# Last stage of a graph kernel: GpSimd turns the sums around, ScalarE works in place

## The chip, the cores and the metric

The kernel runs on one core of a Trainium2 chip. The metric is device time in microseconds (us) of one execution. Five engines are spoken of: TensorE (PE, with its weight loads PEld), VectorE (DVE), ScalarE (ACT), GpSimd (POOL), and SyncE (SP), which here only issues DMAs.

## The reference

For 16 batches b, 1024 nodes u and v and 256 features, the reference computes a gate for every pair of nodes and batch, and sums messages with it:

```
pre_u = einsum('bud,dk->buk', h, W1[:d]);  pre_v = einsum('bvd,dk->bvk', h, W1[d:])
hidden = relu(pre_u[:, :, None, :] + pre_v[:, None, :, :] + b1)
S   = sigmoid(einsum('buvk,ko->buvo', hidden, W2)[..., 0] + b2[0])
a_t = einsum('buv,bud->bvd', S * A, h)
m_t = einsum('uv,bud->bvd', A, h) * h
z_t = beta1 * h + beta2 * (a_t @ Wa + ba) + beta3 * (m_t @ Wm + bm)
```

The adjacency A is sparse (about one pair in sixteen is an edge), so the sum over k is only computed for edges.

## The kernel before

Four stages run one after the other, with barriers between them. A node stage computes per-node rows, the products h·Wa (`hWa_dram`), the terms beta1·h + m_t·Wm + biases (`base_dram`) and, per node and batch, a part u and a part v of the gate's argument (`linear_dram`). A small stage then makes lists of indices. The edge loop (256 blocks) computes for each edge and batch a sum of absolute values and scatters it into `sum_dram`, whose layout is [u, v, b] with the 16 batches innermost. A branch for adjacency matrices with crowded blocks follows, which is skipped with these inputs. The last stage turns the sums into gates and multiplies.

The last stage has 64 steps k: 8 column tiles vt of 128 nodes v, and in each 8 row tiles t of 128 nodes u. A step handles one block of 128 x 128 pairs and all 16 batches:

- SP loads the sums of the block into `raw` (1 MB, [u, v, b]), and a block of adj into `adj_b`. At t = 0 it loads `of_v` first, the part v of the tile, broadcast to all partitions (1 MB). In the first column tile it also loads `hWa_all` (2 MB a step), which then stays. At t = 4 it loads `z` from `base_dram` (2 MB), once the store of the `z` of the column tile before has landed (`z_stored`). SP is one queue in the order of the program: a wait in it holds all loads behind.
- GpSimd adds `of_v` to `raw` in place (L1453), one contiguous instruction over 2048 numbers a partition.
- ScalarE applies the sigmoid with 16 instructions (L1510), one a batch. Each reads `raw[:, :, b]`, 128 numbers that lie 16 numbers (64 bytes) apart, with the scale `half_sign` and the bias `of_u[:, t, b]` from SBUF, and writes `masked[:, b, :]`, 128 numbers in a row.
- VectorE multiplies `masked` by `adj_b` in place (L1471), 2048 numbers a partition.
- TensorE multiplies with 16 matmuls in float32 (L1489; each shows as two MATMUL records), and sums over t in all 8 banks of PSUM (`z_psum`).

After the mask of step t = 1, VectorE adds the eight banks of the column tile before to `z` (L1462, `finish`), and only after that may TensorE begin t = 0 of the new tile in each bank. ScalarE's queue issues the store of `z` after the instructions of t = 3 (`store`, L1501).

The buffers: RAW = 3 `raw` buffers, each free for the next load when ScalarE has read it (`gate_made`); GM = 3 `masked` buffers, each free when TensorE has read it (`step_done`, waited for by ScalarE); ADJ = 5 `adj_b` buffers. `of_u` and `of_v` belong to the last stage, and `of_u` is prepared by one VectorE instruction (L1465) before ScalarE may begin. Between the edge loop and the branch stands `finish_step`: a barrier, 29 semaphores cleared one by one on SP, and a second barrier.

Of the kernel before, what the change touches and what calls it, by code (L numbers as in the profile page):

```python
# [5 lines left out]
def gnn_edges_kernel(nc, x, adj, W1, b1, W2, b2, Wa, ba, Wm, bm, beta1, beta2, beta3, out):  # L6
# [15 lines left out]
    ALU = mybir.AluOpType  # L22
# [4 lines left out]
    P = 128  # L27
# [38 lines left out]
    with ctx:  # L66
# [22 lines left out]
        betas = sb("betas", [P, 4])  # L89
        half_sign = sb("half_sign", [P, 1])  # L90
        work = ctx.enter_context(ExitStack())
        ident = sb("ident", [P, P], scope=work)
# [38 lines left out]
        with ExitStack() as phase:  # L131
# [734 lines left out]
            with ExitStack() as part:  # L866
                at_u = sb("at_u", [P, NBLK], scope=part)
                at_v = sb("at_v", [P, NBLK], scope=part)
                empty = sb("empty", [P, TILES, P], scope=part)
                found = sb("found", [P, TILES, P], scope=part)  # L870
                levels = over_scan[0:1, 0:PASSES]
                most = sb("most", [1, NT + 2], scope=part)
                with nc.Block() as block:
                    @block.gpsimd
                    def _(pool):
                        nc.gpsimd.iota(at_u[:], pattern=[[P, NT], [0, NJ], [UB, 2]], base=-1, channel_multiplier=0,
                                       allow_small_or_imprecise_dtypes=True).then_inc(at_made, 1)
                        nc.gpsimd.iota(at_v[:], pattern=[[0, NT], [VB, NJ], [0, 2]], base=0, channel_multiplier=0,
                                       allow_small_or_imprecise_dtypes=True).then_inc(at_made, 1)
                        nc.gpsimd.iota(levels, pattern=[[SLOTS, PASSES]], base=0, channel_multiplier=0,  # L880
                                       allow_small_or_imprecise_dtypes=True).then_inc(at_made, 1)
# [11 lines left out]
                    def _(dve):  # L893
# [17 lines left out]
                        dve.wait_ge(at_made, 3)  # L911
                        link_idx(STT(out=at_u[:], in0=at_u[:], scalar=float(N), in1=at_v[:], op0=ALU.mult, op1=ALU.add))
                        dve.wait_ge(flipped, 1)
                        for k in range(2):
                            turned_ = wide[:, k * SLOTS:(k + 1) * SLOTS].rearrange("p (t n) -> p t n", t=TILES)
                            base_ = at_u[:, k * P:(k + 1) * P].rearrange("p (a n) -> p a n", a=1).broadcast_to([P, TILES, P])
                            link_idx(TS(empty[:], turned_, 0.0, FAR, ALU.is_equal, ALU.mult))
                            link_idx(TT(found[:], turned_, base_, ALU.add))
                            link_idx(TT(found[:], found[:], empty[:], ALU.add))
                            link_idx(nc.vector.tensor_copy(idx_all[:, :, k * P:(k + 1) * P], found[:]))  # L920
                        left_indices(dve, link_idx, left_found, left_u[:], left_v[:], left_at[:], left_base[:], LEFT)
# [7 lines left out]
                    def _(sp):  # L929
# [26 lines left out]
        scattered = [sem(f"scattered{i}") for i in range(RING_S)]  # L956
        edge_sems = [*v_loaded, *u_loaded, *pick_loaded, filled_d, filled_a, drained_d, drained_a, left_set, left_added,
                     left_d, left_a, left_totalled, *first_loaded, signed, totalled, mixed_done]

# [20 lines left out]
        def left_step(n):  # L980

            return n // SPAN - 1, n % SPAN

        with ExitStack() as phase:
# [22 lines left out]
            with nc.Block() as block:  # L1007
                @block.sync
                def _(sp):
# [33 lines left out]
                    for n in range(n_blk):  # L1043
                        waits(sp, filled_d, ND * n)
                        waits(sp, filled_a, NA * n)
                        if n + PKS - 1 < n_blk:
                            load_pick(n + PKS - 1)
                        if n >= VG:
                            k, jj = (n - 1) // VG + 1, (n - 1) % VG
                            if k % ST == TURN * jj and k < ST * NGRP:  # L1050
                                load_v(k, jj)
                        if n % VG == 0 and n // VG + 1 < n_blk // VG:
                            load_u(n // VG + 1)
                    for i in range(RING_S):
                        sp.wait_ge(scattered[i], 16 * TILES * ((n_blk - i + RING_S - 1) // RING_S))
# [122 lines left out]
                def _(pool):  # L1178
# [34 lines left out]
                    for n in range(n_blk):  # L1213
# [31 lines left out]
                        for t in range(TILES):  # L1245
                            col = block_of(*blocks[n])
                            scatter(total[slot][:, t, :], idx_all[:, t, col:col + 1], scattered[slot])
            finish_step(edge_sems)

# [140 lines left out]
        with ExitStack() as phase:  # L1390
            RAW, GM, ADJ = 3, 3, 5
            hWa_all = sb("hWa_all", [P, NT, B, D], scope=phase)
# [3 lines left out]
            z = sb("z", [P, B, D], scope=phase)  # L1396
            of_u = sb("of_u", [P, NT, B], scope=phase)
            of_v = sb("of_v", [P, P, B], scope=phase)
            z_psum = [pb(f"z_psum{i}", [P, BANK], scope=phase) for i in range(B // 2)]
# [3 lines left out]
            u_ready = sem("u_ready")  # L1403
            of_u_loaded = sem("of_u_loaded")
            of_v_loaded = sem("of_v_loaded")
            raw_added = sem("raw_added")
# [18 lines left out]
            with nc.Block() as block:  # L1425
                @block.sync
                def _(sp):
                    sp.dma_start(of_u[:], linear_dram[0, :, :].rearrange("(t p) b -> p t b", p=P)).then_inc(of_u_loaded, 16)  # L1428
                    for vt in range(NT):
                        for t in range(NT):  # L1430
                            k = vt * NT + t
                            if t == 0:
                                waits(sp, raw_added, k)
                                sp.dma_start(of_v[:].rearrange("p v b -> p (v b)"), linear_dram[1, vt * P:(vt + 1) * P, :]  # L1434
                                             .rearrange("(a v) b -> a (v b)", a=1).broadcast_to([P, P * B])).then_inc(of_v_loaded, 16)
                            waits(sp, gate_made, k - RAW + 1)
                            sp.dma_start(raw[k % RAW][:], sum_uv[t * P:(t + 1) * P, vt * P:(vt + 1) * P, :]).then_inc(raw_loaded[k % RAW], 16)
# [9 lines left out]
                def _(pool):  # L1447
                    for vt in range(NT):
                        pool.wait_ge(of_v_loaded, 16 * (vt + 1))
                        for t in range(NT):  # L1450
                            k = vt * NT + t
                            pool.wait_ge(raw_loaded[k % RAW], 16 * (k // RAW + 1))
                            nc.gpsimd.tensor_tensor(raw[k % RAW][:], raw[k % RAW][:], of_v[:], ALU.add).then_inc(raw_added, 1)  # L1453

# [43 lines left out]
                def _(act):  # L1498
# [5 lines left out]
                    for vt in range(NT):  # L1504
                        for t in range(NT):
                            k = vt * NT + t
                            act.wait_ge(raw_added, k + 1)
                            step_done(act, k - GM)
                            for b in range(B):
                                last = nc.scalar.activation(masked[k % GM][:, b, :], raw[k % RAW][:, :, b], ACT.Sigmoid,  # L1510
                                                            bias=of_u[:, t, b:b + 1], scale=half_sign[:, 0:1])
# [32 lines left out]
```

## Time and profile before

| | us |
|---|---|
| median of 3 runs | 4033.04 |
| lowest, highest | 4028.12, 4033.12 |
| profiled execution, its own time | 4027.79 |
| its span | 4026.0 |
| PE busy in it | 3470.5 (86%) |
| DVE busy | 2815.8 (70%) |
| ACT busy | 2435.3 (60%) |
| POOL busy | 1837.0 (46%) |

The busy shares are means over stages with different limits. The last stage is what lies behind the first load at 3362.90 us, so 663 us of the span, and is read by itself below. "Idle before" in a row is the time in which the engine did nothing before the instruction, and the arrow names what ended it.

### The profile page before, as it was taken

The page shows a single profiled execution, that of the slowest core. Times are in us where ns is not written, and L with a number is a line of the kernel's source. Part 1 is how long each engine was busy: PE and PEld are TensorE (multiplying, and loading weights), DVE is VectorE, ACT ScalarE, POOL GpSimd, SP SyncE. Part 2 cuts the span into 40 slices and gives each one's busy share as a digit, 9 for nine tenths or more (in the row PEclk, how much of TensorE's full clock was granted, in tenths as well). Part 3 has the DMA queues.
Part 4 walks back from the last instruction along what each step waited for, and adds up shares of the span by engine and source line. Part 5 has one row for each costly group of instructions (what it writes and reads, how often), then busy time and mean ns, then how long its engine had stood idle before and what let it go on. Part 6 is the DMA issues. An engine that isn't in the chain of part 4 may idle for free. (4 is left out here: it accounts for less than half of the span.)

```text
span 4026.0 us, 56126 instructions
## 1 busy us (share of the span) xinstructions
PE 3470.5 (86%) x14232; PEld 2680.2 (67%) x14232; DVE 2815.8 (70%) x4788; ACT 2435.3 (60%) x14050; POOL 1837.0 (46%) x2338
## 2 busy tenths in 40 slices
PE   4977778887878759999999999999999995687877
PEld 2655555555545548887888888888888884566766
DVE  4455655555554359999999999999999993334333
ACT  0111111111111149998999999999999996788786
POOL 2222212212221126666666666666666654554453
PEclk9988989898989879999999999999999997888988
DMA  4455544555555495666757675666666556654643
GB/s 156 176 185 190 194 167 178 207 186 185 194 187 206 156 220 145 138 150 157 170 143 176 145 177 144 160 159 158 152 147 158 140 113 207 226 183 162 213 177 129
DMA packets 342892, 685.83 MB, mean 170 GB/s; under 512 B 38782, under 2 KB 252648, under 8 KB 319720
## 3 DMA queue, kind: packets, MB, share of 16 engines
q1 hardware_dynamic: 304544, 612.07, 52.5%
q0 software_dynamic: 21504, 53.31, 4.4%
q10 hardware_dynamic: 16512, 16.78, 1.2%
q8 instruction: 116, 1.90, 0.2%
q14 instruction: 216, 1.77, 0.2%
HBM read 444.01 MB, written 256.18 MB: 174 GB/s over the span
## 5 line engine op out<-in xcount | busy, mean ns | idle before, releaser
L1160 ACT ACTIVATE junk<-psum_a 128x128 f32<-128x128 f32 x6144 | 1611.3, 298 | 233.1 <-PE psum_a L1064 149.8
L1160 ACT ACTIVATION_READ_ACCUMULATOR junk<-psum_a 128x1 f32 x6144 | 1385.1, 228 | 0.0
L1105 DVE TENSOR_REDUCE group_sum<-psum_d 128x56 f32<-128x896 f32 x1024 | 1112.6, 1086 | 84.3 <-PE psum_d L1064 41.6
L1063 PE MATMUL psum_d<-u_t,pk 128*128 128x512 f32 x2560 | 1007.3, 393 | 58.9 <-DMA v_t<-rows_dram 33.3
L1064 PE MATMUL psum_d<-v_t,pk 128*128 128x512 f32 x2560 | 1001.2, 391 | 0.0
L1489 PE MATMUL z_psum<-hWa_all,masked 128*128 128x256 f32 x2048 | 486.4, 402 | 183.5 <-DVE masked L1471 128.1
L1209 POOL DMA_INDIRECT sum_dram<-total,idx_all x512 | 506.9, 990 | 228.0 <-POOL total L1220 124.1
L1063 PE MATMUL psum_a<-u_t,pk 128*128 128x512 f32 x1536 | 606.8, 395 | 0.0
L1063 PEld LDWEIGHTS psum_d<-u_t,pk 128*128 128x128 f32 x2560 | 483.0, 189 | 182.2 <-issue 46.2
L1064 PE MATMUL psum_a<-v_t,pk 128*128 128x512 f32 x1536 | 600.0, 391 | 0.0
L1489 PEld LDWEIGHTS z_psum<-hWa_all,masked 128*128 128x128 f32 x2048 | 414.0, 203 | 255.9 <-DVE masked L1471 133.6
L1510 ACT ACTIVATE masked<-raw,of_u,half_sign 128x128 f32<-128x128 f32 x1024 | 510.7, 603 | 116.1 <-POOL raw L1453 78.9
L1064 PEld LDWEIGHTS psum_d<-v_t,pk 128*128 128x128 f32 x2560 | 483.1, 189 | 98.9
L847 POOL TENSOR_TENSOR own<-whole 128x256 f32<-128x256 f32 x128 | 92.6, 724 | 998.2 <-issue 732.2
L601 PE MATMUL wide<-adj_sb,h 128*128 128x512 f32 x1024 | 513.1, 624 | 0.0
L1471 DVE TENSOR_TENSOR masked<-masked,adj_b 128x2048 f32<-128x2048 f32 x64 | 202.5, 3164 | 405.8 <-ACT masked L1510 405.8
L671 ACT COPY hWa<-ring 128x512 f32<-128x512 f32 x64 | 37.5, 587 | 716.1 <-PE ring L623 716.1
L1453 POOL TENSOR_TENSOR raw<-raw,of_v 128x2048 f32<-128x2048 f32 x64 | 303.9, 4764 | 333.4 <-DMA raw<-sum_dram 333.4
L1202 POOL TENSOR_TENSOR fold<-group_sum,group_sign 128x256 f32<-128x256 f32 x256 | 190.2, 743 | 390.9 <-DVE group_sum L1132 387.8
L585 PE MATMUL ring<-W_k,hT 128*128 128x258 f32 x1024 | 276.6, 430 | 104.7 <-ACT whole L664 103.2
L1102 DVE TENSOR_REDUCE late_sum<-psum_d 128x4 f32<-128x512 f32 x512 | 348.0, 680 | 0.8 <-PE psum_d L1064 0.8
L1063 PEld LDWEIGHTS psum_a<-u_t,pk 128*128 128x128 f32 x1536 | 289.4, 188 | 78.9 <-ACT junk L1160 21.4
(207 smaller groups left out, 4049.8 us busy)
## 6 DMA issues: line engine op xcount, KB each, us to landing
u_t<-rows_dram SPq DMA_DIRECT2D x126, 1024.0 KB
rows_dram<-split SPq DMA_DIRECT2D x128, 512.0 KB, 3.3
sum_dram<-zero SPq DMA_DIRECT2D x128, 512.0 KB, 4.9
pk<-pick_dram SPq DMA_DIRECT2D x512, 128.0 KB
raw<-sum_dram SPq DMA_DIRECT2D x64, 1024.0 KB, 6.9
v_t<-rows_dram SPq DMA_DIRECT2D x36, 1024.0 KB
whole_dram<-whole SPq DMA_DIRECT2D x128, 256.0 KB, 3.6
pick_dram<-pick SPq DMA_DIRECT2D x128, 256.0 KB, 2.0
```

Source lines behind the costliest of these rows:

```text
L585: last = nc.tensor.matmul(ring[:, w * BANK:w * BANK + CW], hT[:, c, t * P:(t + 1) * P], W1_k[:, c, w, :], start=(c == 0), stop=(c == DT - 1))
L601: last = nc.tensor.matmul(wide[:, c * N + n * BANK:c * N + (n + 1) * BANK], h[b % 2][:, t, c * P:(c + 1) * P], adj_sb[:, t, n * BANK:(n + ...
L1063: nc.tensor.matmul(dst, pk[n % PKS][:, at:at + P], part(u_t[k % 2][:], b, LB), start=True, stop=False)
L1064: return nc.tensor.matmul(dst, pk[n % PKS][:, SLOTS + at:SLOTS + at + P], part(v_t[n % VG][:], b, LB), start=False, stop=True)
L1102: return nc.vector.tensor_reduce(out_, in_, AX, ALU.add, apply_absolute_value=True)
L1105: nc.vector.tensor_reduce(out_[:, :, 1:EG], in_[:, :, GW:LATE].rearrange("p b (g k) -> p b g k", k=GW), AX, ALU.add, apply_absolute_value= ...
L1160: last = nc.scalar.activation(junk[:, a % RING_A, k * LATE:(k + 1) * LATE], psum_a[a % RING_A][:, k * LATE:(k + 1) * LATE], ACT.Abs, accum ...
L1209: nc.gpsimd.indirect_dma_start(out=sum_dram[:, :], out_offset=bass.IndirectOffsetOnAxis(ap=at, axis=0), in_=sums, in_offset=None, bounds_c ...
L1453: nc.gpsimd.tensor_tensor(raw[k % RAW][:], raw[k % RAW][:], of_v[:], ALU.add).then_inc(raw_added, 1)
L1471: nc.vector.tensor_tensor(masked[k % GM][:], masked[k % GM][:], adj_b[k % ADJ][:].rearrange("p (a v) -> p a v", a=1).broadcast_to([P, B, P ...
L1489: last = nc.tensor.matmul(z_psum[b // 2][:, (b % 2) * D:(b % 2 + 1) * D], masked[k % GM][:, b, :], hWa_all[:, t, b, :], start=(t == 0 and ...
L1510: last = nc.scalar.activation(masked[k % GM][:, b, :], raw[k % RAW][:, :, b], ACT.Sigmoid, bias=of_u[:, t, b:b + 1], scale=half_sign[:, 0:1])
```

## The change

The change has three parts.

1. In the last stage GpSimd reads `raw` and `of_v` in the order [b, v] (128 numbers that lie 64 bytes apart, for each of 16 batches), adds them, and writes `masked[:, b, :]` in runs. ScalarE then works in place on `masked`, in rows. A `raw` buffer is free when GpSimd has read it, and there are 2 of them; of `masked` there are 4, and it is GpSimd, not ScalarE, that waits for TensorE to have read the buffer.
2. `of_u` and `of_v` live from the start of the kernel, and SP loads them in the edge loop, eight blocks before its end. To make room in the stage of indices, four temporary tensors there lie in buffers that exist already (`edge`).
3. After the edge loop there is one barrier in place of barrier, clears and barrier.

```diff
+        of_u = sb("of_u", [P, NT, B])
+        of_v = sb("of_v", [P, P, B])
...
+        def load_of_v(sp, vt):
+            sp.dma_start(of_v[:].rearrange("p v b -> p (v b)"), linear_dram[1, vt * P:(vt + 1) * P, :]
+                         .rearrange("(a v) b -> a (v b)", a=1).broadcast_to([P, P * B])).then_inc(of_v_loaded, 16)
...
+                        if n == n_blk - 2 * VG:
+                            sp.dma_start(of_u[:], linear_dram[0, :, :].rearrange("(t p) b -> p t b", p=P)).then_inc(of_u_loaded, 16)
+                            load_of_v(sp, 0)
...
-            finish_step(edge_sems)
+            nc.all_engine_barrier()
...
-            RAW, GM, ADJ = 3, 3, 5
+            RAW, GM, ADJ = 2, 4, 5
...
-                    sp.dma_start(of_u[:], linear_dram[0, :, :].rearrange("(t p) b -> p t b", p=P)).then_inc(of_u_loaded, 16)
                     for vt in range(NT):
                         for t in range(NT):
                             k = vt * NT + t
-                            if t == 0:
-                                waits(sp, raw_added, k)
-                                sp.dma_start(of_v[:].rearrange("p v b -> p (v b)"), linear_dram[1, vt * P:(vt + 1) * P, :]
-                                             .rearrange("(a v) b -> a (v b)", a=1).broadcast_to([P, P * B])).then_inc(of_v_loaded, 16)
-                            waits(sp, gate_made, k - RAW + 1)
+                            if t == 0 and vt:
+                                sp.wait_ge(raw_added, k)
+                                load_of_v(sp, vt)
+                            waits(sp, raw_added, k - RAW + 1)
                             sp.dma_start(raw[k % RAW][:], sum_uv[t * P:(t + 1) * P, vt * P:(vt + 1) * P, :]).then_inc(raw_loaded[k % RAW], 16)
...
                             pool.wait_ge(raw_loaded[k % RAW], 16 * (k // RAW + 1))
-                            nc.gpsimd.tensor_tensor(raw[k % RAW][:], raw[k % RAW][:], of_v[:], ALU.add).then_inc(raw_added, 1)
+                            step_done(pool, k - GM)
+                            nc.gpsimd.tensor_tensor(masked[k % GM][:], raw[k % RAW][:].rearrange("p v b -> p b v"),
+                                                    of_v[:].rearrange("p v b -> p b v"), ALU.add).then_inc(raw_added, 1)
...
                             act.wait_ge(raw_added, k + 1)
-                            step_done(act, k - GM)
                             for b in range(B):
-                                last = nc.scalar.activation(masked[k % GM][:, b, :], raw[k % RAW][:, :, b], ACT.Sigmoid,
+                                last = nc.scalar.activation(masked[k % GM][:, b, :], masked[k % GM][:, b, :], ACT.Sigmoid,
                                                             bias=of_u[:, t, b:b + 1], scale=half_sign[:, 0:1])
```

How the instructions stand on GpSimd at the start of the last stage (the names of the waits are semaphores: `raw_loaded` is a landed load, `gate_used` a step that TensorE has read). Before:

```order
L1446 UNCONDITIONAL_BRANCH
L1453 TENSOR_TENSOR raw<-raw,of_v 128x2048 [waits raw_loaded0,of_v_loaded]
L1453 TENSOR_TENSOR raw<-raw,of_v 128x2048 [waits raw_loaded1]
L1453 TENSOR_TENSOR raw<-raw,of_v 128x2048 [waits raw_loaded2]
L1453 TENSOR_TENSOR raw<-raw,of_v 128x2048 [waits raw_loaded0]
L1453 TENSOR_TENSOR raw<-raw,of_v 128x2048 [waits raw_loaded1]
```

and now, on GpSimd at the same place:

```order
L1449 UNCONDITIONAL_BRANCH
L1457 TENSOR_TENSOR masked<-raw,of_v 128x2048 [waits raw_loaded0,of_v_loaded]
L1457 TENSOR_TENSOR masked<-raw,of_v 128x2048 [waits raw_loaded1]
L1457 TENSOR_TENSOR masked<-raw,of_v 128x2048 [waits raw_loaded0]
L1457 TENSOR_TENSOR masked<-raw,of_v 128x2048 [waits raw_loaded1]
L1457 TENSOR_TENSOR masked<-raw,of_v 128x2048 [waits gate_used,raw_loaded0]
```

The addition now writes `masked`, uses two `raw` buffers in turn, and from the fifth step on also waits for TensorE.

On SP, where the edge loop ends and the last stage begins (the branch that is skipped left out). Before:

```order
L1019 DMA u_t<-rows_dram 64x4096 x2
L1007 UNCONDITIONAL_BRANCH [waits filled_d,filled_a,scattered0,scattered1,scattered2,scattered3,left_scattered]
L83 ISA [waits barrier_Pool_Activation_PE_DVE_SP_release]
L83 ISA x28
L1426 COMPARE_AND_BRANCH [waits barrier_Pool_Activation_PE_DVE_SP_release]
...
L1428 DMA of_u<-linear_dram 128x8x16
L1434 DMA of_v<-linear_dram 128x2048
L1437 DMA raw<-sum_dram 128x2048
L1439 DMA adj_b<-in_adj_dram 128x128
L1441 DMA hWa_all<-hWa_dram 128x16x256
```

and now, on SP at the same place:

```order
L1025 DMA u_t<-rows_dram 64x4096 x2
L1061 DMA of_u<-linear_dram 128x8x16
L987 DMA of_v<-linear_dram 128x2048
L1013 UNCONDITIONAL_BRANCH [waits filled_d,filled_a,scattered0,scattered1,scattered2,scattered3,left_scattered]
L1431 COMPARE_AND_BRANCH [waits barrier_Pool_Activation_PE_DVE_SP_release]
...
L1440 DMA raw<-sum_dram 128x2048
L1442 DMA adj_b<-in_adj_dram 128x128
L1444 DMA hWa_all<-hWa_dram 128x16x256
```

The two loads have moved ahead of the barrier, and the 29 clears and one barrier are gone.

On SP around t = 4 of a later column tile (z is the load that waits for the store). Before:

```order
L1437 DMA raw<-sum_dram 128x2048 [waits gate_made]
L1439 DMA adj_b<-in_adj_dram 128x128 [waits gate_masked]
L1444 DMA z<-base_dram 128x16x256 [waits z_stored]
L1437 DMA raw<-sum_dram 128x2048 [waits gate_made]
L1439 DMA adj_b<-in_adj_dram 128x128 [waits gate_masked]
```

and now, on SP at the same place:

```order
L1440 DMA raw<-sum_dram 128x2048 [waits raw_added]
L1442 DMA adj_b<-in_adj_dram 128x128 [waits gate_masked]
L1447 DMA z<-base_dram 128x16x256 [waits z_stored]
L1440 DMA raw<-sum_dram 128x2048 [waits raw_added]
L1442 DMA adj_b<-in_adj_dram 128x128 [waits gate_masked]
```

The order of the loads is the same; only the semaphore for which the load of `raw` waits is another.

## Rows read from the trace of the kernel before

**Rows 1.** The page's groups of the last stage: form, count, busy, mean ns, idle before.
```profile
L1489 PE MATMUL z_psum<-hWa_all,masked 128*128 128x256 f32 x2048 | 486.4, 402 | 183.5 <-DVE masked L1471 128.1
L1510 ACT ACTIVATE masked<-raw,of_u,half_sign 128x128 f32<-128x128 f32 x1024 | 510.7, 603 | 116.1 <-POOL raw L1453 78.9
L1471 DVE TENSOR_TENSOR masked<-masked,adj_b 128x2048 f32<-128x2048 f32 x64 | 202.5, 3164 | 405.8 <-ACT masked L1510 405.8
L1453 POOL TENSOR_TENSOR raw<-raw,of_v 128x2048 f32<-128x2048 f32 x64 | 303.9, 4764 | 333.4 <-DMA raw<-sum_dram 333.4
```

**Rows 2.** Timeline of ScalarE's queue: three of the stores. Start, us, instruction.
```profile
3488.51 0.42 ACTq L1501 DMA_DIRECT2D out_dram<-z  x1
...
3959.29 0.38 ACTq L1501 DMA_DIRECT2D out_dram<-z  x1
...
4018.13 0.38 ACTq L1501 DMA_DIRECT2D out_dram<-z  x1
```

**Rows 3.** Busy time in one cycle of eight steps.
```profile
core 0: us, PE busy (x) PEld busy (x) DVE busy (x) ACT busy (x) POOL busy (x), PEclk, DMA share, GB/s
3800.20:3878.80 78.60, 60.44 (x258) 51.52 (x257) 30.56 (x16) 63.80 (x129) 38.28 (x8) 0.89 0.51 181
```

**Rows 4.** Timeline of that cycle, all engines: start, us, instruction, count, idle before.
```profile
3800.19 2.58 ACT L1510 ACTIVATE masked<-raw,of_u,half_sign 128x128 f32<-128x128 f32 x5 [5.31 <-PE z_psum L1489]
3802.30 0.38 ACTq L1501 DMA_DIRECT2D out_dram<-z  x1
...
3809.81 0.37 SPq L1444 DMA_DIRECT2D z<-base_dram  x1
...
3821.10 13.47 POOL L1453 TENSOR_TENSOR raw<-raw,of_v 128x2048 f32<-128x2048 f32 x3 [24.77 <-DMA raw<-sum_dram]
3825.65 47.85 ACT L1510 ACTIVATE masked<-raw,of_u,half_sign 128x128 f32<-128x128 f32 x96 [9.51 <-POOL raw L1453]
...
3834.60 0.32 SPq L1434 DMA_DIRECT2D of_v<-linear_dram  x1
...
3841.67 2.29 DVE L1471 TENSOR_TENSOR masked<-masked,adj_b 128x2048 f32<-128x2048 f32 x1 [4.95 <-ACT masked L1510]
...
3842.16 10.71 POOL L1453 TENSOR_TENSOR raw<-raw,of_v 128x2048 f32<-128x2048 f32 x2 [7.59 <-DMA raw<-sum_dram]
...
3849.67 5.34 DVE L1471 TENSOR_TENSOR masked<-masked,adj_b 128x2048 f32<-128x2048 f32 x1 [5.71 <-ACT masked L1510]
...
3855.07 7.17 PE L1489 MATMUL z_psum<-hWa_all,masked 128*128 128x256 f32 x32 [1.41 <-DVE masked L1471]
...
3878.79 2.58 ACT L1510 ACTIVATE masked<-raw,of_u,half_sign 128x128 f32<-128x128 f32 x5 [5.29 <-PE z_psum L1489]
```

**Rows 5.** Other groups of ScalarE and GpSimd, before the last stage.
```profile
L1173 ACT ACTIVATE left_junk<-left_rows 128x128 f32<-128x128 f32 x192 | 62.3, 357 | 0.0
L1206 POOL TENSOR_TENSOR one<-two 128x32 f32<-128x32 f32 x264 | 63.4, 240 | 20.7
L1220 POOL TENSOR_TENSOR total<-one,late_sum 128x32 f32<-128x32 f32 x256 | 64.9, 253 | 21.1 <-DMA sum_dram<-total,idx_all 0.9 <-POOL one L1206 0.3
```

**Rows 6.** Timeline from the end of the edge loop to the last addition of tile 0.
```profile
3352.84 0.98 POOL L1209 DMA_INDIRECT sum_dram<-total,idx_all  x1 [0.30 <-issue]
...
3363.95 1.16 SPq L1437 DMA_DIRECT2D raw<-sum_dram  x1
...
3373.47 4.49 POOL L1453 TENSOR_TENSOR raw<-raw,of_v 128x2048 f32<-128x2048 f32 x1 [19.65 <-DMA raw<-sum_dram]
...
3440.80 4.53 POOL L1453 TENSOR_TENSOR raw<-raw,of_v 128x2048 f32<-128x2048 f32 x1 [4.27 <-DMA raw<-sum_dram]
```

**Rows 7.** Busy time while `hWa_all` is loaded, columns as above.
```profile
3377.00:3445.00 68.00, 44.37 (x179) 37.15 (x180) 15.21 (x7) 57.48 (x113) 32.44 (x8) 0.81 1.07 364
```

**Rows 8.** The page's DMA issues: size of one, median us from issue to landing.
```profile
raw<-sum_dram SPq DMA_DIRECT2D x64, 1024.0 KB, 6.9
```

More of the change, by code:

```diff
@@ L866, in gnn_edges_kernel @@
             with ExitStack() as part:
[L867 to L870, printed above, removed]
+                at_u, at_v = edge[0][:, 0:NBLK], edge[0][:, NBLK:2 * NBLK]
+                empty = edge[1][:, 0:SLOTS].rearrange("p (t n) -> p t n", t=TILES)
+                found = edge[1][:, SLOTS:2 * SLOTS].rearrange("p (t n) -> p t n", t=TILES)
                 levels = over_scan[0:1, 0:PASSES]
@@ L875, in _ @@
                     def _(pool):
-                        nc.gpsimd.iota(at_u[:], pattern=[[P, NT], [0, NJ], [UB, 2]], base=-1, channel_multiplier=0,
+                        nc.gpsimd.iota(at_u, pattern=[[P, NT], [0, NJ], [UB, 2]], base=-1, channel_multiplier=0,
                                        allow_small_or_imprecise_dtypes=True).then_inc(at_made, 1)
-                        nc.gpsimd.iota(at_v[:], pattern=[[0, NT], [VB, NJ], [0, 2]], base=0, channel_multiplier=0,
+                        nc.gpsimd.iota(at_v, pattern=[[0, NT], [VB, NJ], [0, 2]], base=0, channel_multiplier=0,
                                        allow_small_or_imprecise_dtypes=True).then_inc(at_made, 1)
@@ L911, in _ @@
                         dve.wait_ge(at_made, 3)
-                        link_idx(STT(out=at_u[:], in0=at_u[:], scalar=float(N), in1=at_v[:], op0=ALU.mult, op1=ALU.add))
+                        link_idx(STT(out=at_u, in0=at_u, scalar=float(N), in1=at_v, op0=ALU.mult, op1=ALU.add))
                         dve.wait_ge(flipped, 1)
@@ L916, in _ @@
                             base_ = at_u[:, k * P:(k + 1) * P].rearrange("p (a n) -> p a n", a=1).broadcast_to([P, TILES, P])
[L917 to L920, printed above, removed]
+                            link_idx(TS(empty, turned_, 0.0, FAR, ALU.is_equal, ALU.mult))
+                            link_idx(TT(found, turned_, base_, ALU.add))
+                            link_idx(TT(found, found, empty, ALU.add))
+                            link_idx(nc.vector.tensor_copy(idx_all[:, :, k * P:(k + 1) * P], found))
                         left_indices(dve, link_idx, left_found, left_u[:], left_v[:], left_at[:], left_base[:], LEFT)
@@ L956, in gnn_edges_kernel @@
         scattered = [sem(f"scattered{i}") for i in range(RING_S)]
-        edge_sems = [*v_loaded, *u_loaded, *pick_loaded, filled_d, filled_a, drained_d, drained_a, left_set, left_added,
-                     left_d, left_a, left_totalled, *first_loaded, signed, totalled, mixed_done]
         UNITS_D = [[("e", 0), ("e", 1), ("l", 3)], [("e", 0), ("e", 1), ("l", 3)]]
@@ L982, in left_step @@
             return n // SPAN - 1, n % SPAN
+        of_u_loaded = sem("of_u_loaded")
+        of_v_loaded = sem("of_v_loaded")
+        def load_of_v(sp, vt):
+            sp.dma_start(of_v[:].rearrange("p v b -> p (v b)"), linear_dram[1, vt * P:(vt + 1) * P, :]
+                         .rearrange("(a v) b -> a (v b)", a=1).broadcast_to([P, P * B])).then_inc(of_v_loaded, 16)
         with ExitStack() as phase:
@@ L1396, in gnn_edges_kernel @@
             z = sb("z", [P, B, D], scope=phase)
-            of_u = sb("of_u", [P, NT, B], scope=phase)
-            of_v = sb("of_v", [P, P, B], scope=phase)
             z_psum = [pb(f"z_psum{i}", [P, BANK], scope=phase) for i in range(B // 2)]
@@ L1403, in gnn_edges_kernel @@
             u_ready = sem("u_ready")
-            of_u_loaded = sem("of_u_loaded")
-            of_v_loaded = sem("of_v_loaded")
             raw_added = sem("raw_added")
```

## The prediction

> **What bounds the kernel now.** I read the page's groups first, then the busy time of one stretch of the last stage, then the timeline of the same stretch, since all that the change touches on purpose lies in the last 663 us. In the groups [rows 1] ScalarE is the busiest of the four engines of this stage, 510.7 us, with little idle time; GpSimd is busy 303.9 us and idle for 333.4 us, waiting for loads of `raw`; VectorE waits for ScalarE for 405.8 us. The stage repeats every eight steps: the stores of `z` at 3488.51 and 3959.29 are six cycles apart [rows 2], so a cycle is 78.46 us. In one cycle ScalarE is busy for 63.8 us, TensorE for 60.4, VectorE for 30.6, GpSimd for 38.3, and the DMA engines for half of it [rows 3]. No engine is full: the cycle is a chain, and the timeline [rows 4] shows its links. ScalarE begins t = 3 at 3800.19, and the store of `z` is issued at 3802.30 (2.1 us). It lands after 7.5 us, which releases the load of `z` at 3809.81. The load of `raw` for t = 5 stands behind that one on SP, and both land so that GpSimd begins at 3821.10 (11.3 us). GpSimd's addition takes 4.5 us, and then ScalarE runs 96 instructions, six steps, in 47.85 us (7.97 us a step, 498 ns apart). It then waits 5.3 us for TensorE's t = 0, to have a free `masked` buffer. 2.1 + 7.5 + 11.3 + 4.5 + 47.85 + 5.3 = 78.6. GpSimd has slack (24.8 us idle before 3821.10), ScalarE has none.
>
> The same rows hold a second thing that the change will meet. VectorE's mask at 3841.67 takes 2.29 us. GpSimd's two additions from 3842.16 take 10.71 us, not 2 x 4.5, and the mask at 3849.67 takes 5.34 us. The two do not run at once: each waits for the other, and where GpSimd runs without a pause a mask puts about 2.3 us between its additions.
>
> **The change, part by part.** Everything hangs on p, the time of GpSimd's new addition, 64 of them. It reads two operands of 2048 numbers at 64 bytes apart where it read them in a row. No row of this kernel shows that on GpSimd. From below: the old addition, 13.47 / 3 = 4.5 us [rows 4]; its own additions of 32 numbers take 240 ns where one operand steps by 8 bytes and 253 ns in a row [rows 5], so a small step is free. A gain on reading is excluded, as the same numbers are read. From above: ScalarE's instruction that reads at 64 bytes takes 603 ns, one of the same shape that reads in a row 357 ns [rows 1, 5], 1.92 ns more per number, which also holds the other function and the operands from SBUF. If each of GpSimd's 4096 reads cost that much more, p = 12.4 us. I take half of it as the part of the stride, 0.96 ns, which gives 6.5 us if only one of the two reads shows and 8.4 us if both do, and between the two p = 7.4 us.
>
> The Trainium skill (GPSIMD Engine Reference, section Performance pitfalls for Q7 kernels) says that GpSimd reads at a step of more than 8 bytes cost about 2.9 cycles a number in place of 1.9. The trace agrees at 8 bytes, where the step is free, and shows nothing beyond. By that ratio p would be 6.9 us and the kernel about 4053; by one more cycle at 1.2 GHz for each of both reads, 7.9 us and about 4106. These are estimates.
>
> The new cycle, if GpSimd paces it, counted from the end of its t = 7: `of_v` and `raw` land, 7.6 us (its idle time before 3842.16 [rows 4]; `of_v` can't be loaded earlier, since there is one buffer); four additions, 4p; the masks of t = 0 and 1 between them, 2 x 2.3; then ScalarE begins t = 3 and issues the store, 2.1; the store lands, 7.5; `z` and `raw` land, 11.3 (the addition of t = 4 is hidden there); three additions, 3p, with one mask between, 2.3. Sum 35.4 + 7p. With p = 7.4 it is 87.2 us, 8.7 more than 78.46. The waits that go: ScalarE's 5.3 us for TensorE is hidden, because GpSimd's t = 4 is what waits for TensorE now (GM = 4), and it has 20.9 us. The earlier release of `raw` buys nothing in this cycle, as the load of t = 5 waits for the store, not for a buffer. What ScalarE gains by reading in a row lies beside GpSimd's additions: nothing, as long as its step is shorter than p. Six cycles: +52.4.
>
> Head. From the last scatter's issue at 3352.84 to the load of `raw` at 3363.95 pass 11.1 us [rows 6] with a landing, two barriers, 29 clears and two issues. How much goes isn't shown: between 1 us (the two issues) and 6. I take 3.6. From there to the first addition pass 9.5 us, with `raw` behind 1 MB of `of_v`, which at 364 GB/s [rows 7] is 2.9 us. So the first addition is 6.5 us earlier. Tile 0 is bound by loads, 3 MB a step (8.6 us at 364 GB/s, DMA share above 1), and the additions, p + 2.3 = 9.7 us apart, are now a little slower: 7 x 9.7 = 68 us from the first to the eighth, for 67.3 before (3373.47 to 3440.80 [rows 6]). The eighth ends at 3367.0 + 68 + 7.4 = 3442.4, and the first store follows 7.6 + 4p + 4.6 + 2.1 = 43.9 later, at 3486.3 for 3488.51: -2.2. The early load of 1 MB stands on SP behind all other loads of the edge loop, so nothing waits behind it: 0. The tensors of the index stage: same instructions, 0.
>
> Tail. Before, 68.5 us from the last cycle's store (3959.29 [rows 2]) to the execution's own 4027.79. Now 7.5 + 11.3 + 3p + 2.3 = 43.3 to the end of GpSimd, about 7 for ScalarE, 2.3 for the mask, 7.2 for TensorE (row at 3855.07 [rows 4]), 0.7 for the last bank, and the 9.7 us from the store at 4018.13 to the end: 70.2, +1.7.
>
> Sum: 4027.8 - 2.2 + 52.4 + 1.7 = 4079.7, so 4080. The profiled execution lies 5 us (0.13%) under the median of the runs, within their spread, and I leave it at that. A microsecond of p is worth about 42 us in the six cycles, and with head and tail 49 to 56. The break-even is at p = 6.4 us; p = 6.5 gives about 4033 and p = 8.4 about 4133.
>
> **The rivals.**
> *The stride is nearly free for GpSimd (faster).* For it: the free step of 8 bytes [rows 5], and GpSimd's slack of 333 us [rows 1]. Against: ScalarE's long instruction. With p = 4.5 the chain of GpSimd is 35.4 + 31.6 = 67.0 us. ScalarE's is the old one without the 5.3: 73.3 if it gains nothing, and less than 67.0 once its step is below 6.9 us; TensorE's 60.4 fits in. So 5.2 to 11.5 a cycle, 31 to 69 in six; head about -13, since the first store comes earlier too, and the tail up to -6: 3940 to 3984, say 3960. With two `raw` buffers the landing (6.9 us in the median [rows 8]) is longer than an addition, and could give some back. The Trainium skill (ScalarE: Activation LUTs, section What ACT_TABLE_LOAD costs) puts an activation of 128 numbers with two operands from SBUF at 479 ns and the overlap of neighbours at 93; the trace has 603 ns and 105. By it ScalarE's step would fall to 6.2 us, and this rival would end at GpSimd's 67.0.
> *Each read pays the full difference (much slower).* p = 12.4: 122.2 a cycle, +262 in six, and about 60 in head and tail: near 4350. Even p = 9 gives 4165. Against: the 1.92 ns is only partly stride.
> *The gain and the loss cancel.* p between 6.2 and 6.6: within 8 us of 4028.
>
> **How the numbers follow.** Forecast, slower by a p between 6.6 and 8.9: 0.46, 4080, its own range 4036 to 4160. p above that: 0.12. Free or nearly free stride (p up to 5.2): 0.29. p from 5.2 to 6.2, a small gain: 0.07. Cancelled: 0.06. What a measurement can tell is 0.2%, 8 us. Faster 0.36, the same 0.06, slower 0.58. The range for 8 in 10 leaves out the far end of the slow side and a little of the fast: 3955 to 4160.
>
> **What would show it.** The mean of the new addition decides: over 6.4 us it is slower. In the profile after, GpSimd should be busy for about 64 x (7.4 + a mask's share), over 500 us, its idle time near 150, and ScalarE should wait for GpSimd in most steps; the stores should be 87 us apart. ScalarE's mean should fall below 603 ns, to between 357 and 500. A mask should stand behind an addition and take up to p + 2.3. If GpSimd's mean is near 4.7 us, the step p has failed, and the stores 67 to 73 us apart show the first rival. If the additions are long and the cycle is short, the chain over the store isn't what I take it for. The first addition should begin 4 to 9 us earlier, behind the last scatter.

## The result, and the profile after

The changed kernel takes 4065.89 us (4064.85 to 4067.39, 4 runs), the kernel before 4033.08 us: the ratio is 1.0083, with a 95% interval of 1.0065 to 1.01. It is slower by 33 us; 4080 was forecast. The profiled execution took 4065.12 us.

The page's groups of the last stage after the change, for [rows 1]:

```profile
L1494 PE MATMUL z_psum<-hWa_all,masked 128*128 128x256 f32 x2048 | 485.6, 402 | 222.6 <-DVE z L1467 127.8
L1457 POOL TENSOR_TENSOR masked<-raw,of_v 128x2048 f32<-128x2048 f32 x64 | 514.6, 8067 | 170.9 <-DMA raw<-sum_dram 94.8
L1514 ACT ACTIVATE masked<-masked,of_u,half_sign 128x128 f32<-128x128 f32 x1024 | 401.1, 480 | 269.4 <-POOL masked L1457 269.4
L1476 DVE TENSOR_TENSOR masked<-masked,adj_b 128x2048 f32<-128x2048 f32 x64 | 249.5, 3898 | 400.7 <-ACT masked L1514 400.7
```

GpSimd has taken ScalarE's place as the busiest engine that others wait for: 514.6 us for 303.9. ScalarE gave 110 us of its own time and now waits 269.4 us for GpSimd. The mean of 8067 ns is not the cost of the addition. The view of its line gives the shortest, the median and the longest:

```profile
L1457 POOL TENSOR_TENSOR masked<-raw,of_v x64: 7015/7577/9349, 3365.9 to 4029.1; 128x2048 f32<-128x2048 f32 x64
```

Alone it takes 7.02 us (4.5 before); what lies above is waiting for VectorE's masks. Busy time in the cycle between two stores, for [rows 3]:

```profile
core 0: us, PE busy (x) PEld busy (x) DVE busy (x) ACT busy (x) POOL busy (x), PEclk, DMA share, GB/s
3826.29:3911.39 85.10, 60.57 (x257) 51.62 (x257) 36.18 (x17) 50.13 (x129) 64.67 (x8) 0.84 0.47 167
```

and the timeline of GpSimd, ScalarE, VectorE and SP in it, for [rows 4] (the rows stand engine by engine):

```profile
3828.37 7.28 POOL L1457 TENSOR_TENSOR masked<-raw,of_v 128x2048 f32<-128x2048 f32 x1 [3.79 <-PE z_psum L1494]
3844.85 23.67 POOL L1457 TENSOR_TENSOR masked<-raw,of_v 128x2048 f32<-128x2048 f32 x3 [9.20 <-DMA raw<-sum_dram]
3875.97 33.72 POOL L1457 TENSOR_TENSOR masked<-raw,of_v 128x2048 f32<-128x2048 f32 x4 [7.44 <-issue]
...
3826.29 0.38 ACTq L1506 DMA_DIRECT2D out_dram<-z  x1
...
3868.56 6.26 ACT L1514 ACTIVATE masked<-masked,of_u,half_sign 128x128 f32<-128x128 f32 x16 [2.99 <-POOL masked L1457]
3884.36 6.27 ACT L1514 ACTIVATE masked<-masked,of_u,half_sign 128x128 f32<-128x128 f32 x16 [9.54 <-POOL masked L1457]
...
3858.50 2.92 DVE L1476 TENSOR_TENSOR masked<-masked,adj_b 128x2048 f32<-128x2048 f32 x1 [14.15 <-ACT masked L1514]
3865.68 5.01 DVE L1476 TENSOR_TENSOR masked<-masked,adj_b 128x2048 f32<-128x2048 f32 x1 [4.26 <-ACT masked L1514]
...
3833.82 0.37 SPq L1447 DMA_DIRECT2D z<-base_dram  x1
...
3868.55 0.32 SPq L987 DMA_DIRECT2D of_v<-linear_dram  x1
```

The cycle can be read off: the store lands, 3826.29 to 3833.82 (7.5 us); `z` and `raw` land, to 3844.85 (11.0); three additions, 23.67, which is 3 x 7.02 and 2.6 for a mask; `of_v` and `raw` land, 7.4; four additions, 33.72, which is 4 x 7.02 and 5.6 for two masks; 1.7 to the next store. The sum is 85.1. ScalarE's step is 6.26 us, and before each step it waits. TensorE is busy for 60.57 us of the cycle, for 60.44 before, so the longer cycle is not work of TensorE.

Where the 37.3 us between the two profiled executions lie: the stores, at 3485.54 and 3996.46 for 3488.51 and 3959.29 [rows 2], are six cycles apart, 85.15 us each for 78.46.

| | before | after | difference |
|---|---|---|---|
| to the first store | 3488.51 | 3485.54 | -3.0 |
| six cycles | 470.78 | 510.92 | +40.1 |
| last of these stores to the execution's end | 68.50 | 68.66 | +0.2 |

The head, on GpSimd and SP, for [rows 6]:

```profile
3351.92 0.98 POOL L1218 DMA_INDIRECT sum_dram<-total,idx_all  x1 [0.30 <-issue]
3365.91 7.01 POOL L1457 TENSOR_TENSOR masked<-raw,of_v 128x2048 f32<-128x2048 f32 x1 [13.01 <-DMA raw<-sum_dram]
...
3434.72 7.93 POOL L1457 TENSOR_TENSOR masked<-raw,of_v 128x2048 f32<-128x2048 f32 x1 [1.26 <-DMA raw<-sum_dram]
...
3360.07 0.34 SPq L1440 DMA_DIRECT2D raw<-sum_dram  x1
```

From the last scatter to the first addition are 14.0 us, for 20.6 before.

### The profile page after: what moved, and what is told of

It reads as the page before. It is cut to its first block and busy times, and to the rows that moved or that the text cites. A ratio compares the mean times of both kernels' runs of the same rounds, so it can differ in the third digit from the quotient of the medians.

```text
span 4063.4 us, 56078 instructions
## 1 busy us (share of the span) xinstructions
PE 3463.8 (85%) x14232; PEld 2677.5 (66%) x14232; DVE 2862.4 (70%) x4788; ACT 2319.9 (57%) x14050; POOL 2044.3 (50%) x2338
## 5 line engine op out<-in xcount | busy, mean ns | idle before, releaser
L1457 POOL TENSOR_TENSOR masked<-raw,of_v 128x2048 f32<-128x2048 f32 x64 | 514.6, 8067 | 170.9 <-DMA raw<-sum_dram 94.8
L1514 ACT ACTIVATE masked<-masked,of_u,half_sign 128x128 f32<-128x128 f32 x1024 | 401.1, 480 | 269.4 <-POOL masked L1457 269.4
L1476 DVE TENSOR_TENSOR masked<-masked,adj_b 128x2048 f32<-128x2048 f32 x64 | 249.5, 3898 | 400.7 <-ACT masked L1514 400.7
```

What stands on the lines that cost most here:

```text
L1457: nc.gpsimd.tensor_tensor(masked[k % GM][:], raw[k % RAW][:].rearrange("p v b -> p b v"), of_v[:].rearrange("p v b -> p b v"), ALU.add).th ...
L1476: nc.vector.tensor_tensor(masked[k % GM][:], masked[k % GM][:], adj_b[k % ADJ][:].rearrange("p (a v) -> p a v", a=1).broadcast_to([P, B, P ...
L1514: last = nc.scalar.activation(masked[k % GM][:, b, :], masked[k % GM][:, b, :], ACT.Sigmoid, bias=of_u[:, t, b:b + 1], scale=half_sign[:, ...
```

## The experiments

Each ran beside the kernel before on the same chip; a ratio is to that one. Line numbers of the experiments can differ by a few from those above. A cycle is one sixth of the time between the first and the seventh store.

**The price of a strided read: `both_in_rows` and `one_in_rows`.** A strided read takes numbers that lie apart (here 64 bytes), one in rows takes them one after the other. Both are edits of the changed kernel that leave out all or part of the turn from [v, b] to [b, v]:

```diff
-nc.gpsimd.tensor_tensor(masked[k % GM][:], raw[k % RAW][:].rearrange("p v b -> p b v"), of_v[:].rearrange("p v b -> p b v"), ALU.add)
+# both_in_rows
+nc.gpsimd.tensor_tensor(masked[k % GM][:].rearrange("p b v -> p (b v)"), raw[k % RAW][:].rearrange("p v b -> p (v b)"), of_v[:].rearrange("p v b -> p (v b)"), ALU.add)
+# one_in_rows
+nc.gpsimd.tensor_tensor(masked[k % GM][:], raw[k % RAW][:].rearrange("p v b -> p b v"), of_v[:].rearrange("p v b -> p (v b)").rearrange("p (b v) -> p b v", b=B), ALU.add)
```

> The changed kernel, but GpSimd reads both operands in a row (the numbers land in the wrong place of the gates, so the turn from [v, b] to [b, v] is left out). Theory (the stride alone makes the addition 7.0 us): the addition takes 4.5 us, the cycle falls to 67 us (7.6 + 4 x 4.5 + 4.6 + 2.1 + 7.5 + 11.3 + 3 x 4.5 + 2.3) and the time to about 3942 (3930 to 3965). Rival (it is the write to masked or the other buffer count that costs): the addition stays near 7 us and the time at 4066.

> The changed kernel, but of_v is read in a row and only raw at the stride of 64 bytes (part v is added to the wrong pairs). Theory (each strided read pays the same, 0.61 ns a number): the addition takes 5.8 us, the cycle 76 us, the time about 4004. Rival A (the two reads overlap, and one strided read costs as much as two): 7.0 us and 4066. Rival B (one strided read is hidden): 4.5 us and about 3942.

Measured: 3938.95 us (ratio 0.9784, 0.9768 to 0.98) with both in rows, 3991.46 us (0.9912, 0.9895 to 0.9929) with one. The line of the addition in both (shortest, median, longest), first with both in rows:

```profile
L1457 POOL TENSOR_TENSOR masked<-raw,of_v x64: 4488/4522/6596, 3365.2 to 3898.0; 128x2048 f32<-128x2048 f32 x64
```

and with `raw` alone at the stride:

```profile
L1457 POOL TENSOR_TENSOR masked<-raw,of_v x64: 5506/5547/7607, 3363.7 to 3945.8; 128x2048 f32<-128x2048 f32 x64
```

So the shortest are 4.49, 5.51 and 7.02 us for no, one and two strided reads: the one of `raw` costs 1.02 us (0.50 ns a number), that of `of_v` on top of it 1.51 (0.74 ns). The stride is the whole price, and both reads pay. The cycles are 66.1 and 73.1 us. The first theory stood (67 and 3942 were expected); with one strided read the kernel was 13 us faster than expected, since the read of `raw` costs less than half of the two: 5.5 us for an expected 5.8.

The Trainium skill (GPSIMD Engine Reference, section Performance pitfalls for Q7 kernels) gives about 2.9 cycles a number for about 1.9 where a kernel reads at a step of more than 8 bytes, half as much again. Here the whole instruction became 1.56 times as long with two strided operands and 1.23 times with one, so for the instruction as a whole one strided operand costs less than that ratio and two a little more.

**The mask between the additions: `small_mask`.** The changed kernel, with VectorE's mask cut to one column of 128 (the rest of adj is left out):

```diff
-nc.vector.tensor_tensor(masked[k % GM][:], masked[k % GM][:],
-                        adj_b[k % ADJ][:].rearrange("p (a v) -> p a v", a=1).broadcast_to([P, B, P]), ALU.mult)
+nc.vector.tensor_tensor(masked[k % GM][:, :, 0:1], masked[k % GM][:, :, 0:1],
+                        adj_b[k % ADJ][:, 0:1].rearrange("p (a v) -> p a v", a=1).broadcast_to([P, B, 1]), ALU.mult)
```

> The changed kernel, but VectorE's mask multiplies only the first of 128 columns of each batch (the rest of adj is left out), so that the same instruction is about a tenth as long. Theory (three masks a cycle stand between additions of GpSimd on its chain, 2.3 to 2.7 us each): the mean of the addition falls from 8.07 to about 7.1 us, the cycle from 85.1 to 77 to 79 us, the time to about 4022 (4010 to 4032). Rival (GpSimd's long means are its own, and the mask only waits beside it): the mean stays near 8 us and the time within 8 us of 4066.

Measured: 4012.59 us (ratio 0.9964, 0.995 to 0.9979), a cycle of 77.7 us. The groups of GpSimd and VectorE:

```profile
L1457 POOL TENSOR_TENSOR masked<-raw,of_v 128x2048 f32<-128x2048 f32 x64 | 459.8, 7212 | 172.6 <-DMA raw<-sum_dram 101.7 <-issue 50.3 <-PE z_psum L1494 20.6
L1476 DVE TENSOR_TENSOR masked<-masked,adj_b 128x16 f32<-128x16 f32 x64 | 71.2, 1112 | 522.9 <-ACT masked L1514 522.9
```

GpSimd's own instruction is unchanged, and its mean falls from 8067 to 7212 ns, close to the 7.02 of an undisturbed one. The cycle falls by 7.5 us, for the 6.9 that three masks were priced at. The other way round shows too: a mask of 16 numbers takes between 185 and 4560 ns, 1112 in the mean, since it still waits for an addition. The two instructions exclude each other here; the theory stands.

**The store in the chain: `z_late_after` and `z_late_before`.** One edit, of either kernel:

```diff
-                            if t == 4:
+                            if t == 6:
                                 waits(sp, z_stored, 16 * vt)
                                 sp.dma_start(z[:], base_dram...)
```

> The changed kernel with one edit: z is loaded at t = 6 and not at t = 4, so no load of raw stands behind the store of z. Theory (the cycle is GpSimd's chain, and 20.9 us of it are the store and the landing of z and raw): the 9 us that GpSimd waits at t = 5 go, but two or three masks come to stand between additions instead, at 2.3 to 2.7 us each. The cycle falls from 85.1 to 79 to 82 us, and the time from 4066 to about 4040 (4030 to 4048). Rival (the additions and masks alone pace the stage, and the store chain is hidden): no change, 4066.

> The kernel before with one edit: z is loaded at t = 6 and not at t = 4. Theory (before, the cycle is ScalarE's chain over the store, 78.5 us): the stall of 9.5 us before t = 5 goes, 8 steps of 7.97 us and the wait of 5.3 us for TensorE stay, so the cycle is 69 us; six cycles and the tail give about -65 us, 3968. Rival (the load of z then collides with of_v and raw of the next tile and costs the same there): within 10 us of 4033.

Measured: the changed kernel 4028.11 us (ratio 0.9999, 0.999 to 1.0009), a cycle of 79.6 us, as expected; the time a little below its range, as the wait goes from the last tile too. The kernel before 3969.23 us (0.9849, 0.9832 to 0.9865), a cycle of 70.0 us for an expected 69. ScalarE now runs through a cycle with one wait, here in the kernel before with the edit:

```profile
3771.07 61.53 ACT L1510 ACTIVATE masked<-raw,of_u,half_sign 128x128 f32<-128x128 f32 x123
3839.07 2.59 ACT L1510 ACTIVATE masked<-raw,of_u,half_sign 128x128 f32<-128x128 f32 x5 [6.47 <-PE z_psum L1489]
```

123 instructions without a stall, where [rows 4] had 9.5 us of waiting and then 96. The chain over the store was real in both kernels. It also shows that the cycle is not the sum of busy times: the changed kernel's GpSimd is busier in this experiment (its mean is 8589 ns, more masks between additions) and the kernel faster.

**ScalarE alone: `act_in_rows`.** The kernel before, with ScalarE reading 128 numbers in a row (the turn from [v, b] to [b, v] is left out):

```diff
-raw[k % RAW][:, :, b], ACT.Sigmoid,
+raw[k % RAW][:].rearrange("p v b -> p (v b)")[:, b * P:(b + 1) * P], ACT.Sigmoid,
```

> The kernel before, but ScalarE reads raw in a row and not at a stride of 64 bytes (the gates get the wrong pairs and batches); GpSimd as before. Theory (of ScalarE's 603 ns, 124 are the stride): 479 ns, a step of 6.26 us, the cycle 78.5 - 6 x 1.71 = 68.3 us, the time about 3966. Rival (the wait for TensorE's t = 0 grows by what ScalarE saves): above 4000.

Measured: 3979.4 us (ratio 0.9868, 0.9851 to 0.9884), 13 us above the expected value, and a cycle of 71.5 us for 68.3. The price was right, the use of it was not:

```profile
L1510 ACT ACTIVATE masked<-raw,of_u,half_sign x1024: 477/478/495, 3381.6 to 3959.8; 128x128 f32<-128x128 f32 x171
```

(its line's view: shortest, median, longest), and the group of the last stage:

```profile
L1510 ACT ACTIVATE masked<-raw,of_u,half_sign 128x128 f32<-128x128 f32 x1024 | 399.2, 479 | 179.4 <-POOL raw L1453 126.0 <-PE z_psum L1489 53.4
```

478 ns for 603, 111 us less of ScalarE's time in the stage, of which the kernel gained 50: ScalarE waits 126 us for GpSimd, where it waited 78.9 [rows 1], and 53 for TensorE, where it waited 37. A gain on the engine that paces is kept only until the next link of the chain. Which link it is changes within the run. Four of the six cycles take 68.6 to 70.6 us, near the expected 68.3; the first two take 77.0 and 75.5. ScalarE at t = 3, at the end of one of the first two cycles and of one of the other four:

```profile
3640.11 2.03 ACT L1510 ACTIVATE masked<-raw,of_u,half_sign 128x128 f32<-128x128 f32 x5 [10.21 <-PE z_psum L1489]
...
3709.02 2.03 ACT L1510 ACTIVATE masked<-raw,of_u,half_sign 128x128 f32<-128x128 f32 x5 [3.83 <-PE z_psum L1489]
```

In the long ones it waits over 10 us for TensorE's t = 0, so there the rival came true. TensorE had begun that t = 0 after 6.9 us of idle time at a granted clock of 0.50 (1.2 GHz), and in the short cycle after 3.0 us at 1.00 (2.4 GHz). What tips a cycle one way or the other is not shown.

An estimate from the figures of the Trainium skill (ScalarE: Activation LUTs, section What ACT_TABLE_LOAD costs) puts such an instruction, with both operands from SBUF, at 479 ns; the trace agrees. The 124 ns above it in the mean were the stride, 0.97 ns a number. From start to start, which is what a step of 16 instructions is made of, it is less: 498 ns before and 385 here, 0.88 ns a number.

**The second and third part alone: `early_only`.** The kernel before with `of_u` and `of_v` loaded in the edge loop and one barrier without clears, as in the diff of the change.

> The kernel before with the second and third part of the change alone: of_u and of_v loaded in the edge loop, one barrier without clears after it. Theory: only the head of the last stage moves, by the 6.6 us by which the first addition came earlier in the changed kernel; 4026 to 4028, ratio 0.9984. Rival (tile 0 is bound by loads, and what comes earlier is lost in the queue): 4032.

Measured: 4023.77 us (ratio 0.9986, 0.9977 to 0.9995), which is -5.6 us, with 2 to 9 us inside the interval. The first addition follows the last scatter's issue after 14.0 us:

```profile
3353.55 0.98 POOL L1220 DMA_INDIRECT sum_dram<-total,idx_all  x1 [0.30 <-issue]
3361.70 0.34 SPq L1442 DMA_DIRECT2D raw<-sum_dram  x1
...
3367.50 4.49 POOL L1458 TENSOR_TENSOR raw<-raw,of_v 128x2048 f32<-128x2048 f32 x1 [12.98 <-DMA raw<-sum_dram]
```

This part of the change is a gain, and about as large as expected.

**The two gains together, and the buffers: `best` and `ring_2_4`.** `best` is `early_only` with `z` at t = 6; `ring_2_4` is `best` with

```diff
-            RAW, GM, ADJ = 3, 3, 5
+            RAW, GM, ADJ = 2, 4, 5
```

> The kernel before with the early loads, the one barrier, and z loaded at t = 6. Theory: the two gains add, -65 and -6: about 3961. Rival (the load of z is late for the last tile or collides): 3990 or more.

> The kernel before with early loads, one barrier, z at t = 6 (3966 with 3 and 3 buffers), and now 2 raw and 4 masked buffers: the change's buffer counts under the old division of work. Theory (raw is free only when ScalarE has read it, so landing of 4.8 us and addition of 4.5 us stand against a step of 7.97 us): the wait of 5.5 us for TensorE goes, and a stall of 1.3 us or more a step comes; slower than 3966, 3970 to 4010. Rival (the wait for TensorE was the only one): 3928.

Measured: `best` 3965.84 us (ratio 0.9841, 0.9826 to 0.9856). Beside `z_late_before` on the same chip (0.9849) that is 3 us, less than the 6 expected and within what the intervals allow: that the two gains add in full is not shown. `ring_2_4` 3991.82 us (0.9914, 0.9895 to 0.9931), slower than `best`, as the theory had it: ScalarE no longer waits for TensorE, but 84.7 us of the stage for GpSimd (13.1 in `best`), which waits for loads, and the cycle is 74.4 us for 69.5. Under the old division of work the buffer counts of the change cost about 29 us by the two ratios. The change's own division of work was not run with 3 and 3.

**The turn in the write: `write_strided`.** The changed kernel, with the order of the operands changed so that GpSimd reads in rows and writes at a step of 512 bytes:

```diff
-nc.gpsimd.tensor_tensor(masked[k % GM][:], raw[k % RAW][:].rearrange("p v b -> p b v"), of_v[:].rearrange("p v b -> p b v"), ALU.add)
+nc.gpsimd.tensor_tensor(masked[k % GM][:].rearrange("p b v -> p v b"), raw[k % RAW][:], of_v[:], ALU.add)
```

> The changed kernel, but GpSimd reads raw and of_v in a row, in the order [v, b], and writes masked at a step of 512 bytes; the gates are the same numbers. Theory (only strided reads cost GpSimd time): the addition takes 4.5 us, the cycle 66 us as with both operands and the result in a row, the time about 3939. Rival (a strided write costs what a strided read does, 1 to 1.5 us): 5.5 to 6 us, and 3985 to 4005. Rival (it costs more than both reads, as each number goes to another line): over 7 us and over 4066.

Measured: 3943.83 us (ratio 0.9794, 0.9778 to 0.9811), a cycle of 66.05 us, the same as with both operands and the result in rows:

```profile
L1457 POOL TENSOR_TENSOR masked<-raw,of_v x64: 4514/4549/6632, 3369.4 to 3903.1; 128x2048 f32<-128x2048 f32 x64
```

4.51 us for 4.49: the strided write is all but free where the two strided reads cost 2.5 us. The change was right in what it gives ScalarE, and put the turn on the wrong side of GpSimd's instruction.

**What is left: `write_strided_z_late` and `turn_at_0`.** The first is `write_strided` with `z` at t = 6; the second has one edit more:

```diff
-                            if t == 1 and vt:
+                            if t == 0 and vt:
                                 finish(vt - 1)
```

> The same, and z is loaded at t = 6 and not at t = 4. Theory (the 20.9 us of store and landing leave the chain; what is left is TensorE, 57 to 60 us a cycle, with a pause at the banks' turn): the cycle falls to 61 to 64 us, the time to 3905 to 3925. Rival (GpSimd's additions with masks and the landing of of_v pace it at 66 us): about 3940. If the strided write is slow, GpSimd paces it: 7.6 + 8 p + 6 x 2.5.

> The kernel with the strided write and z at t = 6 (3936), and VectorE adds the banks to z after the mask of t = 0 and not after that of t = 1. Theory (its cycle of 66.6 us is a chain: TensorE's t = 0 to 3, 30.9 us, one addition 4.6, and 31.7 us from the end of the eighth addition over the landing of of_v, two additions, ScalarE's two steps and the mask of t = 1 to TensorE's next t = 0): ScalarE's second step, the second addition's share and the wait for them leave it, 6 to 10 us, and then TensorE's 58.4 us and the turn of a bank pace it at 59 to 61 us; the time 3893 to 3912. Rival (the landing of of_v and the pause of TensorE at the turn are set by something else, such as the store of z): within 8 us of 3936.

Measured: `write_strided_z_late` 3936.27 us (ratio 0.9771, 0.9755 to 0.9788). It was expected at 3905 to 3925 with a cycle of 61 to 64, and the cycle is 66.6: the theory missed. The number is that of the rival (GpSimd's additions and the landing of `of_v`, 66 us and about 3940), but GpSimd is not the engine that paces: it waits for TensorE for 142 us of the stage, where it waited for 43 in `write_strided`. Taking the store out of the chain gave nothing in the cycle, since another chain is as long. Its timeline:

```profile
3735.89 58.38 PE L1493 MATMUL z_psum<-hWa_all,masked 128*128 128x256 f32 x256 [8.70 <-DVE z L1466]
...
3766.80 4.56 POOL L1457 TENSOR_TENSOR masked<-raw,of_v 128x2048 f32<-128x2048 f32 x1 [2.35 <-PE z_psum L1493]
3771.39 0.32 SPq L987 DMA_DIRECT2D of_v<-linear_dram  x1
...
3778.73 14.90 POOL L1457 TENSOR_TENSOR masked<-raw,of_v 128x2048 f32<-128x2048 f32 x3 [7.37 <-DMA raw<-sum_dram]
...
3803.05 3.33 PE L1493 MATMUL z_psum<-hWa_all,masked 128*128 128x256 f32 x7 [8.78 <-DVE z L1466]
```

TensorE runs 58.4 us without a pause and then stands for 8.8, waiting for VectorE's `z`. That stands behind the mask of t = 1, which stands behind two additions and ScalarE's two steps, and those behind the landing of `of_v`, which is issued when the eighth addition has ended at 3771.4. With the sum of the banks moved ahead of t = 1, the kernel takes 3888.15 us (ratio 0.9653, 0.9637 to 0.967), 5 us below its range, with a cycle of 58.9 us. That is 7.7 us less, and not all of it is the shorter wait. TensorE now waits for VectorE's `z` for 2.2 to 3.6 us a cycle, and its unbroken run is itself shorter, 55.5 us in four of the five whole ones (57.2 in the other). One of them, and the group of the whole stage:

```profile
3640.93 55.49 PE L1493 MATMUL z_psum<-hWa_all,masked 128*128 128x256 f32 x256 [2.95 <-DVE z L1466]
...
L1493 PE MATMUL z_psum<-hWa_all,masked 128*128 128x256 f32 x2048 | 454.7, 385 | 73.7 <-DVE masked L1475 50.0 <-DVE z L1466 23.7
```

The run of 55.49 us has a granted clock of 1.00 (2.4 GHz) throughout. The one of 58.38 us above, after a pause of 8.7 us, has 0.50 (1.2 GHz) in its first 4.1 us, then 0.82 from 3740 to 3745, and 1.00 after that. So 58.4 us, on which the theory built its 59 to 61, is not TensorE's own time: the pause costs its 8.7 us and 1.7 to 2.9 us more at the lower clock behind it. 50.0 us of waiting for masks in the stage are left too, but no whole run has such a wait inside it.

`turn_at_0` beats the kernel before by 140 us. It holds all three parts of the change, with the turn in the write, and two edits of place.

## Why the prediction was right

1. *The price p, the time of GpSimd's addition.* 7.4 us, taken between 6.5 and 8.4 as half of the difference between two of ScalarE's instructions. Measured 7.02. The difference of 1.92 ns a number was 0.97 ns of stride (603 for 479 ns in the mean), so halving it was right for ScalarE. For GpSimd the reads cost 0.50 and 0.74 ns, less than the 0.96 that was taken: 6.5 us for one read that shows was too high (5.5), and 8.4 for two (7.0). That the middle of two wide guesses fell within 6% has luck in it: the upper bound, 12.4 us, was far from what happened, and the lower one, 4.5 us, would have turned the sign. The addition of 32 numbers that takes 240 ns has both operands at a step of 8 bytes, not one, so it says a little more than was read in it, and still nothing about 64 bytes. Of the forecast's 15 us too much, p is the largest part: 0.38 us less, at 42 us each in the six cycles, are 16. The other terms of the cycle give back 4, and head and tail take 2.
2. *The cycle, 35.4 + 7p.* With 7.02 it gives 84.5 us; measured 85.15. The links were 7.5, 11.0, 7.4 and 1.7 us for the forecast 7.5, 11.3, 7.6 and 2.1, and the three masks 8.2 us for 6.9: 2.6 to 2.8 us each between two additions, where the shortest mask takes 2.3.
3. *ScalarE's gain is worth nothing here.* Right: its step fell from 7.97 to 6.26 us, its mean from 603 to 480 ns, as the range 357 to 500 had it, and it waits 269 us for GpSimd.
4. *The wait for TensorE moves to GpSimd and hides.* Right in the cycle: GpSimd waits 3.8 us for it before t = 4, within the 18.6 us that the store and the landing take.
5. *The head.* The first addition was to follow 6.5 us sooner; it did by 6.6 (14.0 for 20.6). 3.7 of them are the landing without `of_v` (5.8 us for 9.5, forecast 2.9), 3.0 the barrier, the clears and the issues (forecast 3.6, a guess between 1 and 6), so two misses cancel. The eighth addition was forecast to end at 3442.4 and ended at 3442.65. `early_only` gives the part alone, -5.6 us, of which 3.3 show at the first store (3485.21 for 3488.51).
6. *The tail.* +1.7 forecast, +0.2 measured.
7. *The rivals.* The nearly free stride was put at 3940 to 3984, and `both_in_rows` (3939) shows what it would have been, at its fast end, for the reason given: GpSimd's chain of 67.0 us (66.1 measured), not ScalarE's. It had 0.29 of the chance. The prediction doesn't have the way to it that keeps the change, with the stride moved to the write.

What stays open: why the second strided read costs more than the first, and why a write at 512 bytes costs next to nothing. Whether `of_v` alone at the stride would cost what `raw` alone does was not tried, nor a write at another step.

## What to carry to other kernels

Where a layout must be turned on the way through an elementwise GpSimd instruction, try the turn in the write before the turn in the reads: here 0.03 us for 2.53. Moving work from the pacing engine to one with slack is worth what the receiving engine's whole chain allows, not its idle time: GpSimd had 333 us to spare and was still too slow, because its instructions stand in one chain with a store, a landing and VectorE's masks. And look for the wait that closes the cycle: a load that waits for a store, placed two steps later in the queue, gave 60 us in the kernel before, nearly twice what the change lost.

## What the runs showed of the hardware

- GpSimd, float32 addition of 2048 numbers a partition: 4.49 us in rows, 5.51 with one operand read at 64 bytes, 7.02 with both, 4.51 with both in rows and the result written at 512 bytes.
- ScalarE, 128 numbers with scale and bias from SBUF: 479 ns in rows and 603 at 64 bytes in the mean (the shortest 477 and 582), and from start to start 385 and 498.
- GpSimd's addition and VectorE's multiplication of two SBUF operands exclude each other, in both directions: an addition grows from 7.0 to 9.3 us, and a multiplication of 16 numbers from 185 ns to 1112 in the mean.
- TensorE's 256 matmul records of a cycle took 55.5 us at a granted clock of 1.00 throughout, in `turn_at_0` after pauses of 2.2 to 3.0 us, and 57.2 to 58.4 us in `write_strided_z_late` after pauses of 8.7 to 8.8 us, with a clock of 0.50 to 0.57 in the first 4 us. After a pause of 3.6 us in `turn_at_0` it was 57.2 us too, with 0.63 in the first 4.
